# A two-layer graph network on one core: SP copies rows one by one into a staging table, and POOL fetches a group from it in one transfer

## The reference, cut to what matters

```
xl, xr = x @ W_l, x @ W_r                               # layer 0
e      = sum_c(leaky_relu(xl[src] + xr[dst]) * att)      # per edge and head
alpha  = softmax of e over the edges of one dst
x1     = norm(x + norm(sum_dst(alpha * xl[src]) + bias + x) * gamma + beta)
neigh  = sum_dst(x1[src] + edge_attr)                    # layer 1
out    = norm(x1 + leaky_relu((2 * x1 + neigh) @ W1 + b1) @ W2 + b2)
```

## Time and profile before

| What | Value |
|---|---|
| Median of 3 runs | 4096.13 us (4096.04 to 4099.73) |
| The profiled execution, its own time | 4095.71 us |
| Its span, first to last instruction | 4093.7 us |
| Mean granted clock of TensorE | 0.895 of full speed |
| Instructions | 80435 |
| Layer 0, first to last start of a gather | 105.7 to 2064.2 us |
| Layer 1, first to last start of a gather | 2116.6 to 4073.7 us |

### The profile page before, as it was taken

The page is one execution under the profiler, slowest core; times in us unless marked ns, Lnnn a source line. Parts: engine busy times, 40 slices in busy tenths (PEclk is TensorE's granted clock), DMA queues, the critical chain, the costliest instruction groups (busy, mean ns, idle before and its releaser), DMA issues. The chain is left out here.

```text
span 4093.7 us, 80435 instructions
## 1 busy us (share of the span) xinstructions
PE 3047.2 (74%) x19266; PEld 2546.2 (62%) x19267; DVE 2103.7 (51%) x8190; ACT 1600.6 (39%) x3439; POOL 2973.5 (73%) x3194
## 2 busy tenths in 40 slices
PE   6788888888888888888846666666666666666665
PEld 4566666666666666666636666666566656665665
DVE  6577777777777777777743222222322222222222
ACT  4465565555655655565612112121211212111221
POOL 1777777777777777777737777777777777777776
PEclk9899999999999999999978888888888888888888
DMA  6755555555555554555444444444444444444443
GB/s 203 196 141 132 136 138 134 134 133 139 133 136 133 136 136 134 134 132 141 131 84 130 116 118 123 117 118 117 123 117 118 117 122 118 118 117 117 123 117 84
DMA packets 459581, 525.86 MB, mean 128 GB/s; under 512 B 199115, under 2 KB 359287, under 8 KB 459551
## 3 DMA queue, kind: packets, MB, share of 16 engines
q0 software_dynamic: 100352, 208.93, 21.8%
q1 hardware_dynamic: 266498, 268.35, 21.5%
q10 hardware_dynamic: 92701, 48.23, 4.1%
HBM read 471.23 MB, written 53.95 MB: 128 GB/s over the span
## 5 line engine op out<-in xcount | busy, mean ns | idle before, releaser
L1475 POOL DMA_INDIRECT rows<-x_table,src_idx x1568 | 1480.5, 944 | 528.9 <-issue 528.6
L757 POOL DMA_INDIRECT rows<-xl_table,src_idx x1568 | 1482.0, 945 | 488.9 <-issue 465.1
L831 PE MATMUL pA<-wmsg,edge_of 128*128 128x136 f32 x3136 | 408.2, 283 | 133.1 <-DVE edge_of L1166 132.8
L1489 PE MATMUL pA<-edge_of,dst_row 128*128 128x128 f32 x1568 | 314.0, 382 | 238.0 <-DMA rows<-x_table,src_idx 230.5
L831 PEld LDWEIGHTS pA<-wmsg,edge_of 128*128 128x128 f32 x3136 | 381.8, 190 | 144.1 <-issue 141.4
L951 ACT ACTIVATE relu_h<-ph 128x512 f32<-128x512 f32 x392 | 231.1, 597 | 595.8 <-PE ph L789 595.8
L1561 ACT ACTIVATE relu_h<-ph,b 128x128 f32<-128x128 f32 x196 | 71.9, 367 | 977.6 <-PE ph L1525 937.8
L1489 PEld LDWEIGHTS pA<-edge_of,dst_row 128*128 128x128 f32 x1568 | 292.8, 288 | 253.5 <-issue 253.1
L789 PE MATMUL ph<-node_of,xr_win 128*128 128x512 f32 x784 | 402.9, 638 | 11.4 <-issue 10.3
L1005 ACT ACTIVATE node_of<-dst_row,first_node 128x1024 f32<-128x1024 int32 x196 | 406.6, 2075 | 4.2 <-DVE first_node L1083 4.2
L1489 PE MATMUL pT<-node_of,dst_row 128*128 128x128 f32 x1568 | 290.8, 362 | 157.4 <-DMA rows<-x_table,src_idx 147.4
(11 more groups left out here) (185 smaller groups left out, 5433.3 us busy)
## 6 DMA issues: line engine op xcount, KB each, us to landing
dst_row<-in_dst SPq DMA_DIRECT2D x196, 513.0 KB
dst_row<-in_edge_attr SPq DMA_DIRECT2D x195, 512.0 KB
rows<-xl_table,src_idx POOLq DMA_INDIRECT x1568
rows<-x_table,src_idx POOLq DMA_INDIRECT x1568
sums_table<-win ACTq DMA_DIRECT2D x196, 68.0 KB
xr_win<-xr_table SPq DMA_DIRECT2D x196, 64.0 KB
relu_h<-x_table SPq DMA_DIRECT2D x196, 64.0 KB
out_x<-relu_h ACTq DMA_DIRECT2D x196, 64.0 KB
```

Source lines behind the costliest of these rows:

```text
L757: pool.indirect_dma_start(rows[s][:, t, 0:DW], None, xl_table[:, :], bass.IndirectOffsetOnAxis(ap=src_idx[s][:, t:t + 1], axis=0))\
L831: ins = pe.matmul(pA[k][:, 0:WC], edge_of[k][:, t, :], w[:, t, :], start=(t == 0), stop=(t == T - 1))
L1475: pool.indirect_dma_start(rows[s][:, t, 0:D], None, x1_table[:, :], bass.IndirectOffsetOnAxis(ap=src_idx[s][:, t:t + 1], axis=0))\
L1489: ins = pe.matmul(bank, m[:, t, :], one_hot[:, t, :], start=(k == 0 and t == 0), stop=(k == 1 and t == T - 1))
```

## The change

Two groups are no longer (wholly) gathered by POOL: group 132 with all eight tiles, and tiles 5 to 7 of group 184, in both layers. Their rows are brought by SP into a staging table in HBM, one row a copy.

- At the start of layer 0 SP loads the indices of these rows into one partition (`load_fetch_idx`, three transfers, 1408 numbers with padding).
- SP's loops over groups are split into three by `turns`. In the first 32 turns it fetches for group 132 and in the next 12 for group 184: in the step of each group, after everything that the step issued before, it loads eight indices into registers and issues eight DMAs from HBM to HBM, each of one row of 528 bytes (layer 0) or 512 (layer 1), at the address in a register, to the next place of `stage0` or `stage1` (`fetch_rows`). Layer 0's copies read `xl_table`, layer 1's `x1_table`, which is complete by then. After 44 turns (176 groups) there are none.
- POOL's loop is split too: turns up to 32, turn 33 written out with group 132 brought by one plain DMA, turns 34 to 45, turn 46 written out with five gathers and one plain DMA of three tiles for group 184, and the rest. `bring_staged` waits for all copies of its part, and the one DMA writes `rows[s][:, lo:hi, 0:width]`: 128 partitions x 8 (or 3) rows, each row a piece of its own, as a row takes 144 places in the buffer.
- In layer 1 POOL also waits that group 128 (180) has been summed before it overwrites the buffer. For group 132 it no longer waits for the indices; SP still loads them.
- `sweep` shares its registers between its parts. The engines other than SP and POOL get the same loops as before.

The core of the diff:

```diff
+FETCH = 8
+BY_SP = ((132, 0, 8), (184, 5, 8))
...
+def turns(eng, lo, hi, stops, turn):
+
+    for part, stop in enumerate(sorted(stops)):
+        with eng.Fori(lo, stop) as j:
+            turn(j, part)
+        lo = stop
+    with eng.Fori(lo, hi) as j:
+        turn(j, len(stops))
...
+        def load_fetch_idx(sp):
+
+            for part, (g, lo, hi) in enumerate(BY_SP):
+                at, n = ([0] + stops)[part] * FETCH * U, P * (hi - lo)
+                sp.dma_start(fetch_idx[:, at:at + n].rearrange("o (p t) -> o p t", t=hi - lo),
+                             bass.AP(a["src"].tensor, g * G + lo, [[G, 1], [T, P], [1, hi - lo]])).then_inc(S("fetch_idx_in"), 16)
...
+        def fetch_rows(sp, regs, table, layer, width, g, back, part):
+
+            at = FETCH * back
+            sp.load(regs, fetch_idx[0:1, bass.ds(g.times(FETCH, -at), FETCH)])
+            for i in range(FETCH):
+                row = sp.snap(regs[i], min_val=0, max_val=nodes - 1)
+                sp.dma_start(bass.AP(stage[layer].tensor, g.times(FETCH * width, (i - at) * width), [[width, 1], [1, width]]),
+                             bass.AP(table.tensor, row * width, [[width, 1], [1, width]])).then_inc(S(f"staged{layer}{part}{i % 4}"), 16)
+
+        def bring_staged(pool, layer, width, g):
+
+            s, (lo, hi), part = g % U, tiles_of_sp[g], list(tiles_of_sp).index(g)
+            at, n = ([0] + stops)[part] * FETCH * U, hi - lo
+            for i in range(4):
+                pool.wait_ge(S(f"staged{layer}{part}{i}"), 16 * fetches[part] // 4)
+            pool.dma_start(rows[s][:, lo:hi, 0:width], bass.AP(stage[layer].tensor, at * width, [[n * width, P], [width, n], [1, width]]))\
+                .then_inc(S(f"gathered{layer}{s}"), 16 * n)
...
                     if not (g.j is None and g.c + AHEAD >= groups):
                         load_sources(sp, g + AHEAD)
-
-                sweep(sp, groups, step, spans)
+                    if g.part is not None and g.part < len(BY_SP):
+                        sp.wait_ge(S("fetch_idx_in"), 16 * idx_loads)
+                        fetch_rows(sp, fetch_regs, xl_table, 0, DW, g, 1, g.part)
+
+                sweep(sp, groups, step, spans, stops=stops)
...
             def _(pool):
-                with pool.Fori(0, groups // U) as j:
+                def turn(j, skip=None):
                     for s in range(U):
-
-                        wait_alone(pool, pool_waits, S(f"src_in0{s}"), j * 16 + 16)
+                        lo, hi = tiles_of_sp[skip] if skip is not None and skip % U == s else (T, T)
+                        if (lo, hi) != (0, T):
+                            wait_alone(pool, pool_waits, S(f"src_in0{s}"), j * 16 + 16)
                         wait_alone(pool, pool_waits, S(f"rows_free0{s}"), j + 1)
-                        for t in range(T):
+                        for t in [t for t in range(T) if not lo <= t < hi]:
                             pool.indirect_dma_start(rows[s][:, t, 0:DW], None, xl_table[:, :],
                                                     bass.IndirectOffsetOnAxis(ap=src_idx[s][:, t:t + 1], axis=0))\
                                 .then_inc(S(f"gathered0{s}"), 16)
+                        if hi > lo:
+                            pool.wait_ge(S(f"rows_free0{s}"), skip // U + 1)
+                            bring_staged(pool, 0, DW, skip)
+
+                first = 0
+                for skip in tiles_of_sp:
+                    with pool.Fori(first, skip // U) as j:
+                        turn(j)
+                    turn(skip // U, skip)
+                    first = skip // U + 1
+                with pool.Fori(first, groups // U) as j:
+                    turn(j)
```

More of the change, by code:

```diff
@@ L87, in node_loop, with sweep, part, walk @@
     steps(None, range(pairs, pairs + max(lag for _, lag in stages)))
[L90 to L98, removed]
+def turns(eng, lo, hi, stops, turn):
[5 more added lines that the diff above has]
+        turn(j, len(stops))
+def sweep(eng, groups, step, ends=None, layer=0, back=1, stops=()):
+    pool = []
+    def part(j, first, steps, lo, n, turn_part=None):
+        while len(pool) < 2 * n:
+            pool.append(eng.alloc_register(f"ends{layer}_{len(pool)}"))
+        regs = pool[0:2 * n]
+        eng.load(regs, ends[0:1, bass.ds(2 * first if j is None else j * (2 * U), 2 * n)])
         for c in steps:
[L100 to L104, removed]
+            step(Group(j, c, part=turn_part), lambda g: (regs[2 * (g.c - lo)], regs[2 * (g.c - lo) + 1]))
+    part(None, 0, range(back), 0, max(2, back))
+    turns(eng, 0, groups // U - 1, stops, lambda j, k: part(j, 0, range(back, U + back), 0, U + max(2, back), k))
     base = groups - U
-    part("tail", None, base, range(base + back, groups + back), base, U)
-def walk(eng, tag, groups, step, back, extra=0, wants=()):
+    part(None, base, range(base + back, groups + back), base, U)
+def walk(eng, tag, groups, step, back, extra=0, wants=(), stops=()):
     loops = (groups - back) // U
     pool = []
-    def part(j, steps, last):
+    def part(j, steps, last, turn_part=None):
         held, used = [], 0
@@ L132, in part @@
         for c in steps:
-            step(Group(j, c), near)
+            step(Group(j, c, part=turn_part), near)
     part(None, range(back), back)
-    with eng.Fori(0, loops) as j:
-        part(j, range(back, back + U), back + U)
+    turns(eng, 0, loops, stops, lambda j, k: part(j, range(back, back + U), back + U, k))
     part(None, range(back + U * loops, groups + extra + back), groups + extra + back)
@@ L1458, in step @@
                         load_window(g + -2, near(0, g + -2)[0])
-                walk(sp, "sp1", groups, step, BACK, EXTRA, [(starts, 1, 2, windows)])
+                    if g.part is not None and g.part < len(BY_SP):
+                        fetch_rows(sp, fetch_regs, x1_table, 1, D, g, BACK, g.part)
+                walk(sp, "sp1", groups, step, BACK, EXTRA, [(starts, 1, 2, windows)], stops)
                 def load_left(start, n, n16):
@@ L1469, in _, with turn @@
             def _(pool):
-                with pool.Fori(0, groups // U) as j:
+                def turn(j, skip=None):
                     for s in range(U):
-                        wait_alone(pool, pool_waits, S(f"src_in1{s}"), j * 16 + 16)
-                        for t in range(T):
+                        lo, hi = tiles_of_sp[skip] if skip is not None and skip % U == s else (T, T)
+                        if (lo, hi) != (0, T):
+                            wait_alone(pool, pool_waits, S(f"src_in1{s}"), j * 16 + 16)
+                        for t in [t for t in range(T) if not lo <= t < hi]:
                             pool.indirect_dma_start(rows[s][:, t, 0:D], None, x1_table[:, :],
@@ L1477, in _ @@
                                 .then_inc(S(f"gathered1{s}"), 16)
+                        if hi > lo:
+                            pool.wait_ge(S("neigh_summed"), skip + 1)
+                            bring_staged(pool, 1, D, skip)
+                first = 0
+                for skip in tiles_of_sp:
+                    with pool.Fori(first, skip // U) as j:
+                        turn(j)
+                    turn(skip // U, skip)
+                    first = skip // U + 1
+                with pool.Fori(first, groups // U) as j:
+                    turn(j)
             @block.tensor
```

25 lines of the change are left out of this document (22 added, 3 removed).

## The result

The change made the kernel slower: 4592.36 us median (4590.05 to 4594.53) against 4096.48 us for the kernel before on the same chip, a ratio of 1.1209 [1.1196, 1.1223]. 4078.8 us was forecast, 4073 to 4110 the range. The profiled execution took 4590.05 us, its span is 4588.2.

What follows compares the result with a forecast made beforehand. POOL's gathers, 1.249 us each, were taken as the bound. Saving 2 x 8.65 = 17.3 us off 4095.71 gave 4078.4, plus 0.4 for the median 4078.8; range 4073 to 4110.

Steps and rivals of the forecast that it cites:

- What is added to SP: SP's steps of 176 groups a layer: register load and eight copies, 0.95 + 8 x 0.62 = 5.9 us a group.
- the 0.62 us of a copy: SP's time per one-row copy: 0.33 DMA as at L570, the rest register work including 0.09 for an extra instruction.
- two ends for POOL's transfer: Plain POOL transfers: large 1.25 to 7.85 us, small 1.25 to 3.13; 3.1 and 2.0 taken.
- The idle time of 6.3 us a group: SP's waits in layer 0, (1004.9 + 226.7) / 196; the added 5.9 us was to fit with 0.4 to spare.
- the point of 0.67 to 0.73 us a copy: Copy price in layer 0 above which SP decides: 0.67 us from idle time, up to 0.73 from one turn's idle stretches.
- Rival (b): SP becomes the bound; at 0.80 us a copy layer 0 loses 90 to 185 us: 4180 to 4270; chance 0.20.
- the forecast's three signs of being wrong: POOL's gathers idle for src_idx, POOL's turn over 39.95 us, or the first plain transfer busy over 6 us.
- the lower end: POOL's plain transfer costs one instruction like a gather, 0.944 + 0.30 = 1.25 us, whatever its pieces.
- Rival (a): POOL's transfers above about 6.8 and 2.7 us: 4088 to 4096; chance 0.14, including consumers not following.
- its cheap end: Gain per layer with the cheapest plain POOL transfers: 11.2 us, where 8.65 was taken.
- No new wait for the indices: POOL after group 132: indices issued 12.8 us early less 2.2 landing, so no wait was charged.
- layer 0's consumers follow: Layer 0's consumers can gain 0.17 us a group, 8.7 us from group 133 to 184, enough for the 6.9 saved.

Runs made afterwards that it cites:

- the kernel with the copies alone: SP makes layer 0's copies as in the change, POOL gathers everything, layer 1 as before: 4624.05 us beside 4097.26 for the kernel before.
- the kernel with six copies: Against the change, layer 0 has six copies of 144 numbers a group instead of eight of 132: 4086.89 us, ratio 0.9956 to the kernel before.

## Why the prediction was wrong

**The step that failed** is in "What is added to SP": the 0.62 us of a copy. Its register part, 0.29, was right (0.27). Its DMA part, 0.33 from the loads at L570, was not: a row from HBM to HBM took 0.766 us in layer 0 and 0.520 in layer 1. All the 0.33 rows are loads from HBM to SBUF over 128 partitions, and the only one shown of few pieces, ACT's 0.45 us for a single number, was explained away by ACT's first microseconds. The bound from above was missing: the forecast had two ends for POOL's transfer, where at most 16 us hung on it, and one value for the price that is multiplied by 1408.

**The other numbers of SP were good.** The idle time of 6.3 us a group and the point of 0.67 to 0.73 us a copy from which SP decides hold: with copies 0.781 us apart the group took 10.68 us, 0.69 over 9.99, which puts the point at 0.781 - 0.69 / 8 = 0.695. In layer 1 the point was 0.84 and the copies 0.781 apart, so they fit; the waits fell by (1509.7 - 246.5) / 176 = 7.2 us a group, where 0.95 + 8 x 0.781 is 7.2. The register load took 0.67 us in layer 0 and 0.53 in layer 1 (medians), not 0.75. The indices of the copied rows came by two transfers, not three, 1408 numbers without padding; nothing hangs on it.

**Rival (b) happened**, with its mechanism and in its place, at a price of 1.04 us instead of 0.80. Its own working with that price, (0.95 + 8 x 1.04 - 6.3) x 176 = 523 us, comes near the 500 measured; its range, 4180 to 4270, stopped far short. Two of the forecast's three signs of being wrong showed: idle time of POOL put down to src_idx, and 51.6 us a turn (4 x 12.91) where 39.95 was the limit. Its chance of 0.20 rested on a margin of 0.05 us on a price known only from instructions of another kind, which is no ground for odds of four to one.

**The Trainium skill** (page "DMA: Bandwidth & Descriptors", section "Why a DMA increments its semaphore by 16 and not by 1") says that a DMA on fewer than 16 engines leaves the missing increments to the issuing sequencer. It also says that the count of engines is the largest up to 16 that divides the slowest dimension, and that software can split a contiguous row by its largest factor up to 16. The pieces seen here agree: 12 for 132 numbers, 11 for 66, 16 for 128 and 144, one for the prime 131. So do the completion writes: SP's queue has 12 more packets of four bytes for each copy of 132 numbers in the kernel with the copies alone, and not 16. The dearer copies are indeed those below 16, but not in proportion: one piece, with 15 increments missing, costs 0.1 us more and 12 pieces, with 4 missing, 0.25 to 0.3. So no run here shows that these writes are what costs. The prediction had added 0.05 us for it.

**POOL's side.** A gather less gave its 1.25 us. The plain transfer was at the lower end: 1.23 us to the next gather for 1024 pieces and 1.09 for 384, where 3.1 and 2.0 were taken. The Trainium skill, page "DMA: Bandwidth & Descriptors", section "Anatomy of one DMA — SWDGE (gpsimd) path", was held to speak for that end (many descriptors before their cost shows), and the trace agrees: 0.93 us busy for 1024 pieces, 0.79 for 384. Rival (a), dear pieces, is out: layer 1 gained 11.1 us, against 8.65 in the forecast and 11.2 at its cheap end.

**Covers.** "No new wait for the indices" rested on 12.8 us of slack, measured with an SP that had time, less a landing of 2.2 taken from another load; the index loads themselves land 3.2 us after their issue. It held in layer 1 and in the kernel with six copies, and went wherever SP was late (532.8 us). That layer 0's consumers follow could not be seen in the change; with six copies layer 0 gained most of what was asked of it, 8 x 1.249 - 2.2 = 7.8 us: 7.1 by the medians of two kernels, 5.9 by the profile's first to last gather (1952.6 us against 1958.5).

## What to carry to other kernels

Work moved to an engine with idle time is limited by that idle time per step of the loop, not by its share of the span. Divide the one by the number of steps, and where a price is multiplied by more than a thousand, measure it or give it two ends. A DMA's issue time belongs to its form: take it only from rows with the same direction and the same number of partitions or pieces. Padding a row so that its DMA splits in 16 made an issue a third cheaper while moving more bytes. To see which engine bounds a stretch, ask which one waits for nobody in it: here that was SP, though the chain gave it 2%.

## What was not expected of the hardware

- SP's issue of one row from HBM to HBM (what makes 11 and 12 pieces dearer is open): 0.521 us for 512 or 576 bytes (16 pieces), 0.766 for 528 (12 pieces); among mixed widths 0.55 to 0.58, 0.81 to 0.88, and 0.656 for a single piece. The loads of 128 partitions take 0.333.
- A plain transfer of POOL is busy 0.93 us for 1024 pieces and 0.79 for 384; a gather of 128 rows takes 0.944.
- A row split by hand into pieces that lie end to end came out as one contiguous row: 96 pieces of 44 bytes became 16 of 264, issued in 0.571 us.
- Some chips ran every kernel here in about 1.38 times the time, with SP's 33 ns register instructions now and then at 0.7 or 1.4 us. The same edit in layer 1, a gain of 0.3% on a usual chip, lost 5 to 6% there.
